# Join stage of a graph and expert kernel: batch norm by channel, on node features that TensorE has turned

## The reference, cut to what matters

```
out = segment_sum(msg, dst).reshape(N, H * D) + bias          # attention over edges, 8 heads of 32 channels
mean = jnp.mean(out, axis=0)                                   # per channel, over all 3125 nodes
var = jnp.var(out, axis=0)
out = (out - mean) * jax.lax.rsqrt(var + BN_EPS) * gamma + beta
x = x + (out + x_normed)
...
logits = layernorm(x) @ router_w.T                             # 8 experts
```

## Time and profile before

| | |
|---|---|
| time, median of 3 runs | 1950.96 us (1950.69 to 1953.09) |
| time of the profiled execution | 1950.14 us |
| its span, and mean granted PE clock | 1948.4 us, 0.837 |
| busy: PE, PE weight loads, DVE, ACT, POOL | 1389.2, 1156.7, 894.6, 585.7, 1075.6 us |
| join stage, from DVE's first instruction to the router stage's first on DVE | 615.63 to 744.43 us |

### The profile page before, as it was taken

How to read it: one execution, slowest core, us unless ns; L and a number is a source line. 1 busy time by engine, 2 the same in 40 slices (tenths; PEclk the granted TensorE clock), 3 DMA queues, 4 the chain that set the end, 5 groups by cost and what they waited for, 6 DMA issues and landing times. The chain is left out here.

```text
span 1948.4 us, 24181 instructions
## 1 busy us (share of the span) xinstructions
PE 1389.2 (71%) x6890; PEld 1156.7 (59%) x6890; DVE 894.6 (46%) x1795; ACT 585.7 (30%) x1276; POOL 1075.6 (55%) x1064
## 2 busy tenths in 40 slices
PE   7636666665665275699999996576565667667998
PEld 5525544453544264699999996454353545446887
DVE  7345543444444777433333334544333333335943
ACT  4144333333432023233333332322222222222310
POOL 1567777777773400665222471177777777773520
PEclk9858888877886565799999998777979787878999
DMA  6578988888886503342111024733333333330002
GB/s 168 149 205 262 303 282 295 285 278 282 274 278 199 127 1 111 105 132 97 46 47 46 29 95 90 189 106 104 106 104 105 106 105 104 105 92 1 0 1 66
DMA packets 156349, 266.75 MB, mean 137 GB/s; under 512 B 26394, under 2 KB 119583, under 8 KB 155205
## 3 DMA queue, kind: packets, MB, share of 16 engines
q1 hardware_dynamic: 106994, 139.15, 23.0%
q0 software_dynamic: 45424, 122.33, 20.8%
q10 hardware_dynamic: 3811, 3.78, 0.8%
HBM read 168.22 MB, written 97.93 MB: 137 GB/s over the span
## 5 line engine op out<-in xcount | busy, mean ns | idle before, releaser
L1204 POOL DMA_INDIRECT sum_rows<-xn_tab,src_e x391 | 373.3, 955 | 175.3 <-issue 118.9
L1229 PE MATMUL bank<-sum_held,sum_hot 128*125 128x256 f32 x976 | 306.7, 478 | 191.7 <-ACT sum_held L1239 188.3
L817 POOL DMA_INDIRECT gat_rows<-xh_tab,src_e x363 | 343.4, 946 | 114.7 <-issue 108.5
L1229 PEld LDWEIGHTS bank<-sum_held,sum_hot 128*125 128x125 f32 x976 | 224.8, 239 | 271.4 <-issue 178.3
L890 PE MATMUL bank<-gat_rows,gat_same 128*128 128x264 f32 x784 | 261.7, 480 | 126.1 <-issue 126.1
L890 PEld LDWEIGHTS bank<-gat_rows,gat_same 128*128 128x128 f32 x784 | 175.6, 243 | 165.6 <-issue 132.6
L1239 ACT COPY sum_held<-sum_rows 128x1024 f32 x122 | 127.4, 1045 | 373.5 <-SPq L1195 341.6
L1916 PE MATMUL bank<-weights,e_xthigh 128*128 x896 | 219.2, 328 | 7.9 <-DVE e_xtlow L2071 5.4
L934 ACT COPY gat_outs<-bank 128x528 f32<-128x528 f32 x196 | 117.3, 598 | 283.7 <-PE bank L890 283.2
L2076 DVE TENSOR_TENSOR e_h<-e_gated,bank 128x342 f32<-128x342 f32 x112 | 57.1, 510 | 261.0 <-ACT e_gated L2009 261.0
L1261 DVE SCALAR_TENSOR_TENSOR res<-bank,prep_inv,res 125x256 f32 x122 | 58.9, 483 | 236.0 <-PE bank L1229 230.3
(11 more groups left out here) (521 smaller groups left out, 2443.9 us busy)
## 6 DMA issues: line engine op xcount, KB each, us to landing
parts<-gat_outs SPq DMA_DIRECT2D x27, 1904.0 KB, 8.1
staged<-w_tab SPq DMA_DIRECT2D x8, 2132.0 KB, 8.2
w_tab<-w_stage SPq DMA_DIRECT2D x16, 682.0 KB, 10.5
w_raw<-in_L_ffn_w_dram SPq DMA_DIRECT2D x16, 640.0 KB
gat_rows<-xh_tab,src_e POOLq DMA_INDIRECT x391, 4.7
sum_rows<-xn_tab,src_e POOLq DMA_INDIRECT x391, 2.7
w_tab<-w_stage SPq DMA_DIRECT2D x8, 768.0 KB, 10.6
weights<-y_tab SPq DMA_DIRECT2D x10, 600.0 KB
```

The costliest lines, as they stand in the source:

```text
L817: pool.indirect_dma_start(out=rows[b % R][:, t, :], out_offset=None, in_=k.xh_tab, in_offset=bass.IndirectOffsetOnAxis(ap=k.src_e[:, b * S ...
L1204: pool.indirect_dma_start(out=rows[:, at // IP % (RING * GPAIRS), at % IP, :], out_offset=None, in_=k.xn_tab, in_offset=bass.IndirectOffse ...
L1229: m = nc.tensor.matmul(k.ps[s][0:P, 0:C], hot[g % 2][:, s, c, :], held[:, s, c, :], start=(c == 0), stop=(c == IP - 1))
```

## The change

- The two halves are still weighed and added by DVE. PE then turns each tile of the sum by plain transposes (L1437 of the changed kernel), and ACT copies it to `turned_x`, [128 channels of a half, 2 halves, 25 tiles, 125 nodes]. A channel is now a partition.
- DVE takes the batch norm's statistics with BN_STATS along the free axis, one body behind (`spreads`), instead of PE's two passes of sums, DVE's subtraction and ACT's squares. Mean, variance, factor (`grow2`) and offset (`lift2`) are small [128, 2] tiles. gamma and beta are loaded as four rows and turned by PE.
- ACT applies factor and offset in place on `turned_x`, 10 Identity activations of 128x625. PE turns each tile back by a matmul with `side`, the identity beside the router's weights (136 columns, two matmuls for each tile, L1449). DVE adds the 256 columns to `k.res` (L1631), copies the 16 columns that are the features' part of the logits (`extra`, L1632) and takes BN_STATS of the tile before. Both halves of `extra` are added to the logits at the end.
- The logits of the old residual (`plain`) are made from `k.res` as it was before the stage: 13 tiles right behind the head part, 2 behind each of bodies 0 to 3, 4 behind body 4. The addition of beta to all of `k.res` is gone.
- On DVE the order is `shares(i)`, `merge(i)`, `peaks(i + 1)`, `spreads(i - 1)`.

```diff
+    XT, SIDE = 4, 128 + NE
+    HEAD_PLAIN, BODY_PLAIN = 13, (2, 2, 2, 2, 0)
...
+            pe.wait_ge(vecs_in, 32)
+            nc.tensor.transpose(k.ps[6][:, 2 * NE:2 * NE + 4], vec_rows[:, :], k.ident[0:4, 0:4]).then_inc(rw_turned, 1)
...
-            for bank, made, tile in ((k.ps[0], joined, main), (k.ps[1], squared, sq)):
-                for t in range(NT):
-                    if t % TB == 0:
-                        pe.wait_ge(made, t // TB + 1)
-                    m = nc.tensor.matmul(bank[0:P, 0:C], k.ones[0:P, 0:P], tile[:, t, 0:C], start=(t == 0), stop=(t == NT - 1))
-                m.then_inc(summed, 1)
...
+            def plain(first, last):
+                for t in range(first, last + 1):
+                    if t < last:
+                        if t >= XR:
+                            pe.wait_ge(scored, t - XR + 1)
+                        for c in range(2):
+                            m = nc.tensor.transpose(plain_bank[t % XR][:, c * P:(c + 1) * P], k.res[:, t, c * 128:(c + 1) * 128], k.ident[0:P, 0:P])
+                        m.then_inc(res_turned, 1)
+                    if t > first:
+                        pe.wait_ge(res_kept, t)
+                        for c in range(2):
+                            m = nc.tensor.matmul(logits[:, (t - 1) * NE:t * NE], xt[:, (t - 1) % XR, c, :], rwt[:, c, :], start=(c == 0), stop=(c == 1))
+                        m.then_inc(scored, 1)
+            plain(0, HEAD_PLAIN)
+            done = HEAD_PLAIN
+            for i in range(BODIES):
+                pe.wait_ge(joined, i + 1)
+                for t in range(i * TB, (i + 1) * TB):
+                    if t >= XT:
+                        pe.wait_ge(x_kept, t - XT + 1)
...
+                    for c in range(2):
+                        m = nc.tensor.transpose(k.ps[t % XT][:, c * P:(c + 1) * P], main[:, t, c * 128:(c + 1) * 128], k.ident[0:P, 0:P])
+                    m.then_inc(merged, 1)
+                plain(done, done + BODY_PLAIN[i])
+                done += BODY_PLAIN[i]
+            plain(done, NT)
+            pe.wait_ge(x_kept, NT)
+            for t in range(NT):
+                if t % TB == 0:
+                    pe.wait_ge(scaled, 2 * (t // TB + 1))
+                if t >= XT:
+                    pe.wait_ge(extras, t - XT + 1)
+                for c in range(2):
+                    m = nc.tensor.matmul(k.ps[t % XT][0:P, c * SIDE:(c + 1) * SIDE], turned_x[:, c, t, :], side[:, c, :], start=True, stop=True)
+                m.then_inc(applied, 1)
...
+            keep_plain(0, HEAD_PLAIN)
+            done = HEAD_PLAIN
+            exps(0)
             for i in range(BODIES):
-                act.wait_ge(centred, i + 1)
-                nc.scalar.activation(sq[:, i * TB:(i + 1) * TB, 0:C], main[:, i * TB:(i + 1) * TB, 0:C], ACT.Square).then_inc(squared, 1)
+                if i < BODIES - 1:
+                    exps(i + 1)
+                for t in range(i * TB, (i + 1) * TB):
+                    act.wait_ge(merged, t + 1)
+                    nc.scalar.copy(turned_x[:, :, t, :], k.ps[t % XT][:, 0:2 * P].rearrange("p (a n) -> p a n", a=2)).then_inc(x_kept, 1)
+                keep_plain(done, done + BODY_PLAIN[i])
+                done += BODY_PLAIN[i]
+            keep_plain(done, NT)
             act.wait_ge(dev, 1)
...
+            act.wait_ge(lifts, 1)
+            for i in range(BODIES):
+                for a in range(2):
+                    of_body = turned_x[:, a, i * TB:(i + 1) * TB, :].rearrange("p t n -> p (t n)")
+                    nc.scalar.activation(of_body, of_body, ACT.Identity, bias=lift2[:, a:a + 1], scale=grow2[:, a:a + 1]).then_inc(scaled, 1)
...
-            v.tensor_tensor(k.res[:, :, :], k.res[:, :, :], beta.rearrange("p (a c) -> p a c", a=1).to_broadcast([P, NT, C]), ALU.add)
...
+            def spreads(i):
+                dve.wait_ge(x_kept, (i + 1) * TB)
+                for a in range(2):
+                    of_body = turned_x[:, a, i * TB:(i + 1) * TB, :].rearrange("p t n -> p (t n)")
+                    for b, cols in enumerate((slice(0, HALF), slice(HALF, TB * P))):
+                        at = (2 * i + b) * 6
+                        m = v.bn_stats(bs[:, a, at:at + 6], of_body[:, cols])
...
-                me(dve, v.tensor_tensor(feat, feat, over(var[:, :]), ALU.mult))
-                v.tensor_tensor(k.res[:, tiles, :], k.res[:, tiles, :], feat, ALU.add).then_inc(grown, 1)
...
+            for t in range(NT + 1):
+                if t < NT:
+                    dve.wait_ge(applied, t + 1)
+                    both = k.ps[t % XT][0:P, 0:2 * SIDE].rearrange("p (a c) -> p a c", a=2)
+                    rows = k.res[:, t, :].rearrange("p (a c) -> p a c", a=2)
+                    v.tensor_tensor(rows, both[:, :, 0:128], rows, ALU.add).then_inc(grown, 1)
+                    v.tensor_copy(extra[:, t, :, :], both[:, :, 128:SIDE]).then_inc(extras, 1)
+                if t:
+                    dve.wait_ge(grown, t)
+                    m = v.bn_stats(k.stats[:, t - 1, :], k.res[:, t - 1, :])
+            me(dve, m)
```

More of the change, by code:

```diff
@@ L1341, in join_phase @@
             sem(n) for n in ("turned", "drops", "factors", "spread", "scanned", "back", "rows_made"))
-        vecs_in, beta_kept, gaps, weights, joined, summed, centred, squared, dev, root = (
-            sem(n) for n in ("vecs_in", "beta_kept", "gaps", "weights", "joined", "summed", "centred", "squared", "dev", "root"))
+        vecs_in, gaps, weights, joined, merged, x_kept, dev, root, lifts, scaled, applied = (
+            sem(n) for n in ("vecs_in", "gaps", "weights", "joined", "merged", "x_kept", "dev", "root", "lifts", "scaled", "applied"))
         block = ctx.enter_context(nc.Block())
-        sq = chain
         node_rows = k.node_chain.rearrange("(t p) c -> p t c", p=P)
-        beta = k.ps[4][0:P, 0:C]
+        plain_bank = (k.ps[4], k.ps[6], k.ps[7])
         @block.sync
@@ L1434, in _, with keep_plain, exps @@
             nc.scalar.activation(wt_q[:, :, :, :], gap_q[:, :, :, :], ACT.Exp).then_inc(weights_q, 1)
[L1435 to L1438, removed]
+            def keep_plain(first, last):
+                for t in range(first, last):
+                    act.wait_ge(res_turned, t + 1)
+                    if t >= XR:
+                        act.wait_ge(scored, t - XR + 1)
+                    nc.scalar.copy(xt[:, t % XR, :, :].rearrange("p a n -> p (a n)"), plain_bank[t % XR][:, 0:2 * P]).then_inc(res_kept, 1)
+            def exps(i):
                 tiles = slice(i * TB, (i + 1) * TB)
@@ L1474, in _ @@
             dve.wait_ge(rw_turned, 1)
[L1475 removed]
+            v.tensor_copy(rwt[:, :, :], k.ps[6][:, 0:2 * NE].rearrange("p (a e) -> p a e", a=2))
+            v.tensor_copy(side[:, :, 128:SIDE], k.ps[6][:, 0:2 * NE].rearrange("p (a e) -> p a e", a=2))
+            v.tensor_copy(side[:, :, 0:128], k.ident[:, :].rearrange("p (a c) -> p a c", a=1).to_broadcast([128, 2, 128]))
+            me(dve, v.tensor_copy(vecs[:, :, :], k.ps[6][:, 2 * NE:2 * NE + 4].rearrange("p (i a) -> p i a", i=2)))
             dve.sem_inc(rw_ready, 1)
@@ L1551, in _ @@
             peaks(0)
             for i in range(BODIES):
+                shares(i)
+                merge(i)
                 if i < BODIES - 1:
                     peaks(i + 1)
-                shares(i)
-                merge(i)
-            dve.wait_ge(summed, 1)
-            me(dve, v.tensor_scalar(mean[:, :], k.ps[0][0:P, 0:C], 1.0 / N, None, ALU.mult))
-            def over(row):
-                return row.rearrange("p (a c) -> p a c", a=1).to_broadcast([P, TB, C])
-            for i in range(BODIES):
-                feat = main[:, i * TB:(i + 1) * TB, 0:C]
-                v.tensor_tensor(feat, feat, over(mean[:, :]), ALU.subtract).then_inc(centred, 1)
@@ L1577, in _ @@
-            dve.wait_ge(grown, BODIES)
-            norm_stats(k, dve, deviations, roots)
+                if i:
+                    spreads(i - 1)
+            me(dve, spreads(BODIES - 1))
+            counts, means, squares = (bs[:, :, n::3] for n in range(3))
+            per_half = lambda a: a.rearrange("p (a x) -> p a x", x=1).to_broadcast([128, 2, 4 * BODIES])
+            me(dve, v.tensor_tensor(shares2[:, :, :], counts, means, ALU.mult))
+            me(dve, v.tensor_reduce(mean2[:, :], shares2[:, :, :], AX, ALU.add))
@@ L1581, in normed @@
+            me(dve, m)
+            dve.wait_ge(extras, NT)
+            dve.wait_ge(scored, NT)
+            one, two = extra[:, :, 0, :], extra[:, :, 1, :]
+            me(dve, v.tensor_tensor(one, one, two, ALU.add))
+            scores = logits.rearrange("p (t e) -> p t e", e=NE)
+            me(dve, v.tensor_tensor(scores, scores, one, ALU.add))
+            norm_factors(k, dve, deviations, roots)
 def normed(k, out, t):
```

56 lines of the change are left out of this document (23 added, 33 removed).

## The result

The changed kernel takes 1934.51 us (median of 4 runs, 1932.09 to 1937.56) beside 1952.03 us of the kernel before on the same chip: a ratio of 0.9899, 95% interval 0.9882 to 0.9917. Run again later it took 1933.05 us beside 1953.60, ratio 0.9890 (0.9871 to 0.9910). The profiled execution took 1932.46 us, with a span of 1930.4 us and a mean granted PE clock of 0.837, the same clock as before.

What follows compares the result with a forecast made beforehand. The join stage is a chain passing from engine to engine; bodies end 0.4 us later, last sum to router takes 35.9 us, not 56.1, so 19.8 us less: 1950.14 becomes 1930.3, median 1931.1; bounds 1929.7 less 1 us to 1936.

Steps and rivals of the forecast that it cites:

- Head and early logits: Join stage's start: extra DVE copies hidden; 13 logit tiles end at 653.2, making first Exp at most 0.3 us late.
- Bodies: DVE's five rounds of weighing and adding: 7.7 us each from body 2 on, last sum at 688.7, before 688.3.
- their balance: In the bodies: the new order of work gains 5.4 us, and the BN_STATS spend it.
- Statistics and table load: Between last sum and scaling: variance at 695.3, table load ends at 696.3, so the root waits 1 us for ACT.
- drain at each switch: Before the root: a skill's rule adding about 1.38 us per ACT table switch; root 1.4 us later, estimate 1932.5.
- Apply loop: PE turning tiles back and DVE adding them: 0.85 us a tile at a mixed PE clock, 20.4 us for 24.
- The rival of the high level "at once": Apply loop: PE at 2.4 GHz throughout, DVE's 0.79 us a tile, 1.4 us less, 1929.7; chance 0.12.
- Tail: After the last tile: additions, small operations and root to 724.3; router stage at 724.6, 19.8 us earlier.
- the rival of the low level: Apply loop: PE at 1.2 GHz throughout, 3.1 us more, 1934.2; chance 0.18.
- The round trip: Apply loop: four banks fail to decouple the engines, 1.9 us a tile, 25 us more, 1956; chance 0.03.
- The late body: Bodies: Exp late behind copies by 0.5 to 1 us each, or BN_STATS dearer, 3 to 5 us, about 1935; chance 0.10.
- The last two rivals: Apply loop as a round trip, chance 0.03; no gain to speak of, by an unseen cost, chance 0.02.

Runs made afterwards that it cites:

- e1: The changed kernel with `peaks(i + 1)` put ahead of `shares(i)` and `merge(i)` again; 1933.74 us, ratio 0.9913.
- e3: The kernel before with only `peaks(i + 1)` moved behind `merge(i)`; 1948.21 us, ratio 0.9988.
- e2: The changed kernel with all logits of the old residual behind the last body, none in the head or between bodies; 1955.32 us, ratio 1.0020.
- e7: The changed kernel with one bank in place of four in the apply loop, on a slower chip; 2307.46 us, ratio 1.0111.
- e5: The changed kernel with three old-logit tiles behind bodies 0 to 3, and ACT alternating 16-column copies with scalings, on a slower chip; ratio 0.9973.
- e8: The changed kernel with PE, not DVE, adding the weighed halves by accumulating identity products, on the same slower chip as e5; ratio 0.9963.
- e4: The changed kernel with three old-logit tiles behind bodies 0 to 3, and the 16-column copies on ACT behind all ten scalings; 1931.43 us, ratio 0.9896.
- e12: The kernel of e5 with PE, not DVE, adding the weighed halves by accumulating identity products, on a normal chip; 1935.37 us, ratio 0.9902.

## Why the prediction was right

The forecast of 1931.1 us was 3.4 below the first median and 2.0 below the second, inside its range. It was worked out from a median before of 1950.96, and the one beside the result is 1.1 higher: as a gain, 19.8 us were forecast, and 17.5 and 20.6 measured. The stage was forecast at 109.0 us (615.63 to 724.6) and took 107.28 and 107.70. Step by step, with the 0.54 us subtracted by which the new trace starts the stage later:

| step | forecast | measured |
|---|---|---|
| first `shares`, and wait before `peaks(1)` | 653.4, none | 653.45, none |
| four BN_STATS | 1.6 | 1.63 |
| end of the last sum | 688.7 | 688.5 |
| end of the root's table load | 696.3 | 696.2 |
| first tile on DVE | 700.4 | 700.35 |
| last tile on DVE | 720.8 | 718.6 |
| router stage | 724.6 | 722.9 |

- **Head and early logits.** Right. The 13 tiles were placed "at the latest" from 639.0 to 653.2. On the same clock they began at 636.9, and their last copy ended at 651.5 (652.00 in the new trace), so Exp was not late at all.
- **Bodies.** Right, including what I called their balance: e1 and e3 price the order at 4.2 us within the changed kernel and 2.8 in the kernel before, forecast at 5.4 less 0.8 for the two Exps that nothing hides; in the kernel before, PE's last sums, at a lower clock, take part of it back. e2 shows what I had not said: without the early logits nothing would be left of the gain (what batch norm by channel is worth without the rest was no term of the sum).
- **Statistics and table load.** Right to 0.3 us. The Trainium skill's drain at each switch ("ScalarE: Activation LUTs", "What ACT_TABLE_LOAD costs") would put the root at 698.1; it stands at 696.74, 0.01 us behind the load's end, so the trace does not agree with it here either.
- **Apply loop.** The step that was mis-sized. I took a mixed clock and 0.85 us a tile; the sum had 20.4 us for 24 steps, measured are 18.24, 0.76 each: some four tiles at the low level, then the high one throughout, with DVE at 0.737 rather than the 0.79 of my sum (from start to start 0.32 for the addition, 0.08 for the copy and 0.34 for BN_STATS, where I had 0.35, 0.11 and 0.33). The nearest row, 0.81 at 1300 to 1400, was the wrong guide: PE was busy 63% there, and here 5.00 of 5 us at the low level and 4.97, later 4.30, of 5 at the high one (705 to 710, 713 to 718). That this is why the clocks differ is an argument, and no run tests it. The rival of the high level "at once" lacked only those four tiles. The Trainium skill's "TensorE: Matmul & The Clock Gate", "What's actually happening", lets activity release the throttle; the loop agrees, but the early logits, 14.96 us busy of 15 at 0.50, do not.
- **Tail.** From the last tile's addition to the router stage 4.3 us, 3.8 forecast: two BN_STATS are left at the end rather than one, and the stage's start waits 0.54 us for PE's queue, not 0.33.
- **The overall time.** It came out above the forecast although the stage came out 1.7 us below it. In the traces, the later start of the stage (0.54), the experts' products (1.8) and the stages behind them account for it; none is a step of the sum, which took all of that as unchanged. So the closeness of the total owes something to luck. Read by the total alone, 1934.51 us would have spoken for the rival of the low level, put at 1934.2, and lies outside the 1930 to 1933 of the mechanism that I thought likeliest; only the trace shows that PE was at the high level for most of the loop.
- **The rivals.** The round trip is real at 1.88 us a tile (e7), and does not occur with four banks. The late body did not occur on normal chips, with 1.69 us of room where I had feared -0.3, but an Exp that is late behind the early copies is what e5 to e8's chip shows, in the first body alone, at 13 to 16 us instead of my 3 to 5 for all of them. The last two rivals have 0.05 of the chances together, not the 0.06 of my text.

## What to carry to other kernels

Before tuning a stage's arithmetic, look for a part of its result that depends on data which are there early, and give it to engines that idle: here nothing is left of the gain without the old part of a linear product computed ahead of the new one (e2). Batch norm by channel alone brought no time; what it did was to turn the new part's tiles, which the split needs. When work is put ahead on an engine's queue, what is queued behind it gets its delays too, those that the profile of one chip does not show. When an engine takes over a copy that frees a buffer, its place in that engine's queue decides, and a rewrite that is a gain by busy time can lose by it (e4, e12).

## What I had not expected of the hardware

- PE transposing residual tiles and multiplying them by 8 columns stays at 0.50 for 15 us without a pause (637 to 652); the same PE with products of the identity among them, 9.58 us busy of 10 in e12, is granted 1.00, and in the apply loop it rises within its first 5 us. The kind of product doesn't settle it: in the changed kernel's bodies PE transposes and multiplies by 8 columns too, and is granted 1.00 from 663 to 666 and from 670 to 673, but 0.50 in the later bodies. What decides is open.
- ACT can stand still for up to 10.90 us, and PE for 6.35, in code that has nothing of the kernel to wait for in the profile, on one chip of three.
